# Causal attention and a mixture of experts on one core: attention in blocks of four heads and 512 queries, a select in place of the mask matmul, the residual added at the end, the first eight expert tiles loaded during attention

## The chip, the core and the metric

The kernel runs on one core of a Trainium2 chip. Its engines work side by side and meet through semaphores: PE (TensorE), DVE (VectorE), ACT (ScalarE), POOL (GpSimd) and SP, which issues DMAs. The metric is the device time of one execution in microseconds; several runs are taken and their median is compared. One more execution is taken with the hardware profiler, and all rows below are from it.

## The reference

x is 1024 tokens of 256 numbers, in float32. What is computed:

```python
xn = layernorm(x)
q, k = rope(xn @ wq.T), rope(xn @ wk.T); v = xn @ wv.T      # 16 heads of 16
scores = q @ k.T / sqrt(16), masked with -inf where key > query
attn_out = softmax(scores) @ v, heads joined, @ wo.T
s = softmax(xn @ gate_weight.T)                             # 64 experts
w, e = top_k(s, 8); w = w / sum(w)
moe = sum over the 8 experts: w * (silu(xn @ w_gate[e]) * (xn @ w_up[e])) @ w_down[e]   # inner size 96
out = x + attn_out + moe
```

## The kernel before

**Preparation.** The 1024 tokens are eight tiles (NT) of 128. They are normalised, transposed, and multiplied with the weights of q, k, v and the gate. q and k are rotated, transposed and split into a high and a low part, which SP stores to memory (`store_parts`, once for each half of the tokens) and loads again in another order (`stage`, five DMAs for a head group and half). The 16 heads are four groups (G) of four heads (HG). `qz` and `kz` hold a group's queries and keys with head size, parts and extra rows along the partitions; there are three pairs (SLOTS), so group 3 takes the pair of group 0. `set_ones` and `clear_max_rows` fill the extra rows, of which POOL zeroes the surroundings first (L608).

**Attention.** The maximum of each query's scores is needed before the exponential. It is found by a pass of its own: PE multiplies 128 queries with up to 512 keys (`max_scores`, L832, 192 matmuls), DVE takes the maxima (`use_max`: L1156 with the causal mask added, L1159 where no mask is needed). A transpose and two DVE operations give the negated maxima of one group and half (`use_neg`), and SP writes them as two rows of `qz` (`place_negmax`, L440), so that the score matmul subtracts them itself. The second pass goes by steps of one group and one tile of keys: PE computes keys times queries (`scores`, L851, up to 512 queries a matmul, 192 matmuls), adds a causal mask with a bf16 matmul at each diagonal (L854, 128 of them), ACT takes the exponential (L683) into `probs` (two buffers of four heads and 1024 queries), and PE multiplies with v (`pv`, L873) into two banks (L867 fills them with zeros first). After each group ACT copies the sums out (`att_out`, L691), PE transposes (L883), DVE divides by the row sums (L1180, L1181). Order: all eight key tiles of a group from the last to the first, the diagonal with the smallest width first. `attention_order` deals the maximum units out over the steps; before the first score step it makes all of group 0 and AHEAD = 48 units of work more. All A units (maxima, negations, posts, the routing table's spread, att and out) share three PSUM banks in turn and are used by DVE in the same order.

**Routing.** DVE finds the top 8 (L1061 to L1067), PE counts (`counts`, L810 and L813), DVE makes slot numbers and tile tables, POOL scatters the token rows to `slots` in 64 indirect DMAs (L616). The experts' rows are cut into tiles of 128, in this run 90.

**Transition and experts.** The first half of the output projection (128 of the 256 features) runs in the last group's steps, the second half after it (L939, L944, L1222), and with it x becomes the residual in `x_sb`, which SP stores to `y_acc[0]` (L504). POOL's first addition waits for that store. The tiles' rows lie in the place of `v_aug`, their weights in that of `probs`; the first eight tiles' rows and weights are loaded when those are free, by SP. A tile then goes: transpose (L955), copy on DVE (L1238), gate and up (L964), tanh on ACT (L723), products on DVE (L1242, L1246), down (L971), weighting on ACT (L729), and POOL adds the rows to one of four accumulators in memory by indirect DMA (L627). Each of four result buffers is used again when its addition has landed. At the end SP loads the four accumulators (L526, L530) and DVE sums them (L1270, L1274).

## Time and profile before

| | |
|---|---|
| median of 3 runs | 463.66 us (463.17 to 465.8) |
| profiled execution | 461.81 us |
| its span, first to last instruction | 459.7 us |
| PE busy | 364.3 us, 79% |
| DVE busy | 277.5 us, 60% |
| POOL busy | 238.7 us, 52% |
| ACT busy | 168.8 us, 37% |
| DMA | 92.96 MB, 202 GB/s in the mean |

Busy shares are means over three stages that look quite different; a slice of the page's second part is 11.5 us, a digit is a tenth of it. The digits of PEclk are the granted clock in tenths of 2.4 GHz. Durations of matmuls hold their way through the array, so neighbours overlap: what one costs is read from start to start.

### The profile page before, as it was taken

To read this page: it belongs to the slowest core of one execution; us is meant where nothing else is said; L and a number is where in the kernel's file an instruction comes from. 1 tells how busy PE (TensorE), PEld (TensorE's weight loads), DVE (VectorE), ACT (ScalarE), POOL (GpSimd) and SP (SyncE) were. 2 spreads that over 40 slices of the span, in tenths; PEclk is the share of its full clock that TensorE was granted. 3 is DMA by queue.
4 is the path that set the end of the run, shared out by engine and by line. 5 is a ranking of instruction groups with operands and counts; after the bars stand their busy time and mean duration, and the time that the engine had idled before them with its cause. 6 is when DMAs were issued, how large, how long until landed. Compare 5 with 4: busy or idle time off the path is not lost.

```text
span 459.7 us, 9456 instructions
## 1 busy us (share of the span) xinstructions
PE 364.3 (79%) x2230; PEld 248.4 (54%) x2234; DVE 277.5 (60%) x1083; ACT 168.8 (37%) x413; POOL 238.7 (52%) x194
## 2 busy tenths in 40 slices
PE   2695958599999999989997788887888888778600
PEld 1253625255545545544535777776776777677400
DVE  7783687968777987731404556665656656556506
ACT  1132200036545554666672333333333333333300
POOL 3769060007777777000000577868787877777720
PEclk9898875669999999999999989999999999999955
DMA  6038797373358333000047899999999999999997
GB/s 200 0 127 237 205 193 164 145 283 117 136 178 275 132 131 130 16 3 1 1 116 231 234 276 278 299 283 280 306 301 291 302 307 261 281 289 275 292 256 257
DMA packets 72512, 92.96 MB, mean 202 GB/s; under 512 B 8648, under 2 KB 62504, under 8 KB 72488
## 3 DMA queue, kind: packets, MB, share of 16 engines
q1 hardware_dynamic: 46312, 61.59, 43.1%
q0 software_dynamic: 16032, 22.29, 23.2%
q10 hardware_dynamic: 10144, 8.79, 5.9%
q8 instruction: 11, 0.18, 0.2%
q14 instruction: 13, 0.11, 0.1%
HBM read 58.92 MB, written 33.46 MB: 201 GB/s over the span
## 4 chain that ended last, share of the span: by engine, by line
PE 34%; DMA 25%; DVE 16%; issue 12%; POOL 8%; ACT 3%; DVEq 1%; POOLq 1%; SPq 1%; ACTq 0%
DMA y_acc<-att_raw,dst 19%; PE ps L851 9%; PE ps L832 8%; PE ps L873 7%; POOL y_acc L627 7%; DVE ps L1156 3%; DVE mx_low L1159 3%; DMA probs<-y_acc 2%; PE ps L854 2%; PE ps L776 2%; ACT att_raw L729 1%; ACT probs L683 1%; DMA qk_parts<-probs 1%; DMA kz<-ones 1%; DMA y_acc<-x_sb 1%
## 5 line engine op out<-in xcount | busy, mean ns | idle before, releaser
L627 POOL DMA_INDIRECT y_acc<-att_raw,dst x90 | 139.8, 1553 | 117.6 <-ACT att_raw L729 86.9
L683 ACT ACTIVATE probs<-ps 128x128 f32<-128x128 f32 (+3 forms) x192 | 84.1, 491 | 93.0 <-PE ps L854 91.3
L964 PE MATMUL ps<-att,probs 128*96 128x128 f32 x720 | 95.1, 275 | 4.5 <-issue 2.6
L964 PEld LDWEIGHTS ps<-att,probs 128*96 128x96 f32 x720 | 88.5, 165 | 14.8 <-issue 7.4
L616 POOL DMA_INDIRECT slots<-rows,slot_i x64 | 61.7, 964 | 56.5 <-DVE rows L1094 37.3
L832 PE MATMUL ps<-kz,qz 128*128 128x512 f32 (+3 forms) x192 | 71.2, 441 | 18.9 <-DVE mx_low L1159 10.2
L971 PE MATMUL ps<-probs,hidden_sb 96*128 96x256 f32 x180 | 59.5, 412 | 29.2 <-DVE hidden_sb L1246 25.6
L729 ACT ACTIVATE att_raw<-ps,w_slot 128x256 f32<-128x256 f32 x90 | 42.6, 473 | 83.0 <-DVE dst L1232 52.7
L851 PE MATMUL ps<-qz,kz 128*128 128x128 f32 (+3 forms) x192 | 70.0, 420 | 1.0 <-ACT probs L683 0.6
L1156 DVE CUSTOM_DVE_ANT_0 ps<-ps,mask_qk 128x512 f32<-128x512 f32 (+3 forms) x128 | 61.0, 504 | 10.5 <-PE ps L832 10.2
L832 PEld LDWEIGHTS ps<-kz,qz 128*128 128x128 f32 x192 | 39.2, 213 | 42.1 <-DVE mx_low L1159 21.1
L1230 DVE SCALAR_TENSOR_TENSOR w_junk<-v_aug,tile_exp 128x8 f32<-128x8 f32 x90 | 20.4, 227 | 63.3 <-DMA y_acc<-att_raw,dst 62.6
L1159 DVE TENSOR_REDUCE mx_low<-ps 128x1 f32<-128x512 f32 x64 | 44.1, 689 | 21.1 <-PE ps L832 20.2
L851 PEld LDWEIGHTS ps<-qz,kz 128*128 128x128 f32 x192 | 37.3, 198 | 31.7 <-ACT probs L683 19.6
L971 PEld LDWEIGHTS ps<-probs,hidden_sb 96*128 96x128 f32 x180 | 27.2, 191 | 40.3 <-DVE hidden_sb L1246 36.1
L1238 DVE COPY att<-ps 128x256 f32<-128x256 f32 x92 | 38.9, 424 | 11.3 <-PE ps L955 5.8
L873 PE MATMUL ps<-probs,v_aug 128*32 128x512 f32 (+3 forms) x384 | 40.9, 501 | 0.2 <-ACT probs L683 0.2
L723 ACT ACTIVATE att<-ps 96x128 f32<-96x128 f32 x90 | 24.5, 273 | 41.3 <-PE ps L964 37.4
L955 PE MATMUL ps<-ident,v_aug 128*128 128x128 f32 x184 | 35.2, 274 | 0.0
L854 PE MATMUL ps<-mask_kq,ident_b 128*128 128x128 bf16 x128 | 30.0, 236 | 0.0
L1246 DVE TENSOR_TENSOR hidden_sb<-att,ps 96x128 f32<-96x128 f32 x90 | 25.4, 283 | 4.0
L1242 DVE SCALAR_TENSOR_TENSOR att<-att,ps 96x128 f32<-96x128 f32 x90 | 24.6, 273 | 0.0
(142 smaller groups left out, 314.7 us busy)
## 6 DMA issues: line engine op xcount, KB each, us to landing
probs<-w_gu SPq DMA_DIRECT2D x96, 192.0 KB, 5.3
v_aug<-slots SPq DMA_DIRECT2D x96, 160.0 KB
probs<-w_down ACTq DMA_DIRECT2D x88, 96.0 KB
y_acc<-zero SPq DMA_DIRECT2D x12, 384.0 KB, 4.2
qk_parts<-probs SPq DMA_DIRECT2D x4, 1024.0 KB, 6.2
qz<-qk_parts SPq DMA_DIRECT2D x16, 256.0 KB, 6.9
probs<-y_acc SPq DMA_DIRECT2D x3, 1024.0 KB, 8.7
kz<-qk_parts SPq DMA_DIRECT2D x8, 256.0 KB, 5.5
```

The costliest lines, as they stand in the source:

```text
L616: pool.indirect_dma_start(slots[:, :], bass.IndirectOffsetOnAxis(ap=slot_i[:, t, k:k + 1], axis=0), rows[:, t, :], None).then_inc(s_scat, 16)
L627: pool.indirect_dma_start(y_acc[u][:, :], bass.IndirectOffsetOnAxis(ap=dst[u][:, 0:1], axis=0), y_sb[u], None, compute_op=ALU.add).then_in ...
L683: act.activation(probs[:, step % 2, j, lo:hi], ps[:, B_BANKS[n % len(B_BANKS)], lo % HALF:(hi - 1) % HALF + 1], ACT.Exp, scale=DK ** -0.5) ...
L729: act.activation(y_sb[u], ps[:, 4 + b, 0:D], ACT.Copy, scale=w_slot[u][:, 0:1]).then_inc(s_y, 1)
L832: pe.matmul(bank[:, 0:width], head_rows(qz, g, j, i, P), kz[g % SLOTS][0:P, lo // HALF, j, 0:width], start=True, stop=True).then_inc(s_ap, 1)
L851: last = pe.matmul(bank[:, a:b], head_rows(kz, g, j, kt, P), qz[g % SLOTS][0:P, lo // HALF, j, a:b], start=True, stop=True, skip_group_che ...
L854: last = pe.matmul(bank[:, a:a + P], ident_b[:, :], mask_kq[:, :], start=False, stop=True, skip_group_check=True)
L873: last = pe.matmul(ps[VW * j:VW * (j + 1), PV_BANK + lo // HALF, lo % HALF:(hi - 1) % HALF + 1], v_aug[:, kt, g * HG + j, :], probs[:, ste ...
L964: last = pe.matmul(ps[0:I, 2 + b, w * P:(w + 1) * P], wgu[u][:, (2 * c + w) * I:(2 * c + w + 1) * I], xgT[b][:, c * P:(c + 1) * P], start= ...
L971: pe.matmul(ps[:, 4 + b, 0:D], hh[b], wdn[u], start=True, stop=True).then_inc(s_dn, 1)
L1156: dve.tensor_tensor_reduce(bank, bank, mask_qk[:, HALF - width:HALF], 1.0, TAKEN, ALU.add, ALU.max, mx[:, g % 2, i // CT, j, i % CT:i % CT ...
L1159: dve.reduce_max(mx_low[:, g % 2, j, i % CT:i % CT + 1], bank, AX.X).then_inc(s_ad, 1)
```

## The change

- Attention goes by eight blocks of one group and one half of the queries (512), in the order BLOCKS: (0,0), (1,0), (2,0), (0,1), (1,1), (2,1), (3,0), (3,1). A block of half 0 has four key tiles, one of half 1 eight, from the first to the last; 48 steps as before, with the same matmuls for scores and maxima. The sums of a block use one of two banks, alternately, and start with `start=True`, without zeroing.
- The mask matmuls are gone. After the exponentials of a diagonal step POOL sets the future keys to zero in `probs` (`cut_future`), ahead of the scatters in its queue. `pv` of a step comes two steps later (LAG) and waits for the cut. `probs` has four slots of 512 queries.
- The maxima are made 24 units ahead of the scores, growing to 40 units. Projections of v for tiles 2 to 7 come before the first maximum. Top-8 work, counts, ranks and tables are dealt over steps 1 to 22, the scatters over the steps from 12 on.
- The output projection is done with both halves of the features, four tiles in steps 43 to 45, four after the last block. The result is added to `x_sb`, which is no longer stored; DVE adds it to the first accumulator at the end.
- Expert rows and weights get a place of their own, over `qz1` and `kz1`, and the first eight tiles are loaded once block (1,1) is done and all scatters have landed.

```diff
-AHEAD = HG * 12
-FIRST_STEPS = 6
+BLOCKS = ((0, 0), (1, 0), (2, 0), (0, 1), (1, 1), (2, 1), (3, 0), (3, 1))
+AHEAD = 24
 NEG_LAG = 2
+LAG = 2
+P_SLOTS = 4
+CHOOSE_STEP, RANK_STEP, WEIGHT_STEP = 1, 9, 12
+TILE_STEPS = (14, 16, 18, 20, 22)
+OUT_STEP = 43
...
+    for m, (g, c) in enumerate(BLOCKS):
+        units = [("max", g, i, j, u) for i in range(c * CT, (c + 1) * CT) for j in range(HG)
+                 for u in range(len(a_units(i)))]
+        lag = 0 if m == 1 else NEG_LAG
+        if m:
+            units.insert(lag, ("neg",) + BLOCKS[m - 1])
+        stream += units
+    stream.append(("neg",) + BLOCKS[-1])
...
+    for s in range(len(B_STEPS) + LAG):
+        extra = others(s)
+        if s < len(B_STEPS):
             for j in range(HG):
+                n = s * HG + j
+                ahead(AHEAD + n + min(max(n - 32, 0) // 1, 16))
+                order.append(("b", s, j))
+                if j == 1 and s >= LAG:
+                    order.append(("pv", s - LAG))
+                if j % 2 == 1 or s == len(B_STEPS) - 1:
+                    order += extra[:1]
+                    extra = extra[1:]
+            order += extra
+        else:
+            order.append(("pv", s - LAG))
...
@@ SP
             set_ones(0)
+            stage(1, 0)
+            set_ones(1)
             store_parts(1)
             sp.wait_ge(s_parts[1], 32)
             stage(0, 1)
-            stage(1, 1)
-            stage(1, 0)
-            set_ones(1)
             place_negmax(0, 0)
             sp.wait_ge(s_vlog, NT)
             sp.wait_ge(s_rot, NT)
             set_ones(2)
+            stage(2, 0)
+            place_negmax(1, 0)
+            stage(1, 1)
             stage(2, 1)
-            stage(2, 0)
+            place_negmax(2, 0)
+            zero_scratch()
             place_negmax(0, 1)
-            zero_scratch()
...
+            place_negmax(1, 1)
+            sp.wait_ge(s_bp, HG * (last_step(BLOCKS.index((0, 1))) + 1))
+            clear_max_rows(0)
+            stage(3, 0)
+            stage(3, 1)
+            place_negmax(2, 1)
+            place_negmax(3, 0)
+            place_negmax(3, 1)
...
+            sp.wait_ge(s_bp, HG * (last_step(BLOCKS.index((1, 1))) + 1))
             first_tiles = numbers(0)
-            sp.wait_ge(s_pv, (G - 1) * NT + done)
...
-            sp.wait_ge(s_res, NT // 2)
-            sp.dma_start(y_acc[0][0:N, :].rearrange("(t p) d -> p t d", p=P), x_sb[:, :, :]).then_inc(s_resd, 16)
...
@@ POOL
+            def cut_future(s):
+                first = queries(s)[0]
+                diagonal = probs[:, s % P_SLOTS, :, first:first + P]
+                pool.wait_ge(s_be, HG * (s + 1))
+                pool.affine_select(out=diagonal, in_=diagonal, compare_op=ALU.is_ge, fill=0.0, base=0,
+                                   pattern=[[0, HG], [1, P]], channel_multiplier=-1).then_inc(s_cut, 1)
+            pairs = [(t, k) for t in range(NT) for k in range(K)]
+            for s in range(len(B_STEPS)):
+                if on_diagonal(s):
+                    cut_future(s)
...
+                if s >= WEIGHT_STEP:
+                    count = 1 + s % 2 if on_diagonal(s) else 3
+                    for t, k in pairs[:count]:
+                        scatter(t, k)
+                    pairs = pairs[count:]
...
-            pool.wait_ge(s_resd, 16)
...
@@ PE
+            def pv(s):
+                g, c, kt = B_STEPS[s]
+                m = BLOCKS.index((g, c))
+                lo, hi = queries(s)
+                pe.wait_ge(s_be, HG * (s + 1))
+                if on_diagonal(s):
+                    pe.wait_ge(s_cut, cuts_until(s))
+                if kt == 0 and m >= 2:
+                    pe.wait_ge(s_acc, m - 1)
...
-                    if lo == kt * P:
-                        last = pe.matmul(bank[:, a:a + P], ident_b[:, :], mask_kq[:, :], start=False, stop=True,
-                                         skip_group_check=True)
...
@@ DVE
             dve.wait_ge(s_yl[0], 16)
+            link(dve.tensor_tensor(sum_buf(0)[:, :, :], sum_buf(0)[:, :, :], x_sb[:, :, :], ALU.add))
```

## Rows read from the trace of the kernel before

**Rows 1.** The page's second part: granted clock of TensorE in 40 slices.
```profile
PEclk9898875669999999999999989999999999999955
```

**Rows 2.** First score matmul (line L851), then line L832's matmuls up to 96 us.
```profile
L851 PEld LDWEIGHTS ps<-qz,kz x192: 185/190/354, 95.7 to 239.1; 128*128 128x128 f32 x192
...
40.00:96.00 56.00, 29.96 (x62) 15.23 (x62) 0.68 0.76 203
```

**Rows 3.** Attention: length, busy of PE, PEld, DVE, ACT, POOL, clock, DMA.
```profile
93.00:243.00 150.00, 142.32 (x900) 76.05 (x904) 90.22 (x310) 87.38 (x197) 61.67 (x64) 0.97 0.34 116
```

**Rows 4.** POOL's additions: ns shortest/median/longest, first and last start.
```profile
L627 POOL DMA_INDIRECT y_acc<-att_raw,dst x90: 1550/1552/1592, 257.1 to 439.7; - x90
```

**Rows 5.** Timeline of the transition: start us, us, engine, line.
```profile
242.60 1.02 ACT L691 ACTIVATE att_raw<-ps 128x1024 f32<-128x1024 f32 x1 [2.04 <-PE ps L873]
...
251.43 1.08 PE L964 MATMUL ps<-att,probs 128*96 128x128 f32 x8 [0.72 <-DVE x_sb L1222]
...
254.49 0.47 ACT L729 ACTIVATE att_raw<-ps,w_slot 128x256 f32<-128x256 f32 x1 [0.58 <-PE ps L971]
...
257.12 1.59 POOL L627 DMA_INDIRECT y_acc<-att_raw,dst  x1 [73.21 <-ACT att_raw L729]
```

**Rows 6.** Timeline of the start; last two: DMA issues with us to landing.
```profile
40.90 1.10 SPq L413 DMA_DIRECT2D qk_parts<-probs  x2
42.65 3.51 POOL L608 MEMSET kz<- 64x4096 f32 x1 [0.15 <-POOL qz L608]
45.10 1.62 PE L832 MATMUL ps<-kz,qz 128*128 128x512 f32 x3 [4.85 <-DMA kz<-ones]
...
54.56 3.44 PE L776 MATMUL ps<-w_in_sb,xnT 128*128 128x320 f32 x12
...
qk_parts<-probs SPq DMA_DIRECT2D x4, 1024.0 KB, 6.2
...
qz<-neg_hi SPq DMA_DIRECT2D x1, 8.0 KB, 4.9
```

**Rows 7.** DVE's masked maxima: two in the timeline, then all of the line.
```profile
46.63 0.73 DVE L1156 CUSTOM_DVE_ANT_0 ps<-ps,mask_qk 128x512 f32<-128x512 f32 x1
...
47.28 0.73 DVE L1156 CUSTOM_DVE_ANT_0 ps<-ps,mask_qk 128x512 f32<-128x512 f32 x1
...
L1156 DVE CUSTOM_DVE_ANT_0 ps<-ps,mask_qk x128: 288/508/733, 46.0 to 199.0; 128x512 f32<-128x512 f32 x32, 128x384 f32<-128x384 f32 x32, 128x256 f32<-128x256 f32 x32, 128x128 f32<-128x128 f32 x32
```

**Rows 8.** PE in the timeline of attention; last: a product with V, from the chain.
```profile
150.07 0.23 PE L854 MATMUL ps<-mask_kq,ident_b 128*128 128x128 bf16 x1
150.11 0.48 PE L851 MATMUL ps<-qz,kz 128*128 128x512 f32 x1
150.43 0.40 PE L832 MATMUL ps<-kz,qz 128*128 128x512 f32 x1
150.67 0.27 PE L841 MATMUL ps<-ident,mx 128*16 128x128 f32 x1
...
188.73 0.99 PE ps L873 x8
```

**Rows 9.** A group of DVE's top-8 work, 60 to 93 us.
```profile
L1065 DVE FIND_INDEX8 top_i<-top_v,logits 128x8 uint32<-128x64 f32 x8 | 1.7, 218 | 0.0
```

**Rows 10.** Ten microseconds around the first score, columns as in rows 3.
```profile
90.00:100.00 10.00, 9.78 (x33) 5.58 (x33) 7.06 (x20) 2.02 (x7) 0.00 (x0) 0.50 1.02 395
```

**Rows 11.** POOL: the scatters, then the forms nearest to the cut.
```profile
L616 POOL DMA_INDIRECT slots<-rows,slot_i x64: 956/960/1212, 103.0 to 182.9; - x64
...
L583 POOL TENSOR_SCALAR_AFFINE_SELECT mask_qk<-mask_qk 128x512 bf16<-128x512 bf16 x1 | 0.6, 612 | 0.2 <-POOL mask_qk L581 0.2
...
L597 POOL TENSOR_TENSOR qk_rot<-rope_c,rope_s 128x512 f32<-128x512 f32 x8 | 10.4, 1302 | 5.7 <-DVE rope_s L1031 5.6 <-POOL qz L559 0.2
```

**Rows 12.** Timeline of the final sums on DVE.
```profile
448.74 2.29 DVE L1270 TENSOR_TENSOR probs<-probs 128x2048 f32<-128x2048 f32 x1 [11.39 <-DMA probs<-y_acc]
451.75 2.29 DVE L1270 TENSOR_TENSOR probs<-probs 128x2048 f32<-128x2048 f32 x1 [0.71 <-DMA probs<-y_acc]
```

473 lines of the change are left out of this document (203 added, 270 removed).

## The prediction

> **What bounds the kernel now.** I read the page's slices first, for the stages, and then a view of its own for each stage. The reader is to see three stages in them. Up to 95.7 us nothing is near its limit for long: TensorE's granted clock falls to 0.5 again and again [rows 1], and the first score matmul (L851) starts only at 95.7 us, because 62 of the 192 row-maximum matmuls (L832) are made before it [rows 2]. From there to the last product with V at 242.5 us TensorE is busy nearly throughout (142.32 us of the 150 from 93 us on) [rows 3]; DVE, ACT and POOL are not. From 257.1 us POOL adds one expert result after the other: 90 additions, the last issued at 439.7 us, one each 2.05 us, where the issue itself takes POOL 1.55 us, and most of the rest is the time until an earlier addition has landed and frees its buffer [rows 4]. Between the two, from 242.6 to 257.1 us, lies a transition [rows 5]. So the change can save in three places: before 95.7 us, in TensorE's work up to 242.5 us, and in the transition.
>
> **The start.** The first maximum waits for the constant rows, which land at 45.1 us [rows 6]; nothing before that moves. Now the six projections of V that were mixed in come first; three took 3.44 us [rows 6], so six take some 7 us from 40 us on; they are done at about 46.5 us and cost about 1 us beside that wait. Then 16 maxima: DVE takes 0.65 us from start to start for 512 columns (46.63 to 47.28), where the form runs 0.73 us, and its shortest, of 128 columns, 0.29 us [rows 7]; over the four widths I take 0.45 us, together 7 us, to 54 us. Transpose and negation add 1 us. The placement (two small DMAs) then has to pass SP's queue. There one more stage of group 1 and its ones now stand ahead of the second store. The ones wait for POOL's memset of kz1, which ends at 46.2 us [rows 6], so the store's two DMAs leave from 46.9 instead of 40.9 us. Their issue takes 1.1 us and they land 6.2 us later, at 54.2 us. Then five stage DMAs are issued in 2.7 us, and the placement, issued by 57.8 us, lands 4 to 5 us later behind that stage (4.9 us now [rows 6]). First scores: 62 us (58 to 66), 34 us earlier than now. Later placements stand behind stages too, and (0,1) behind the 13 zeroing DMAs (some 0.5 to 1 us of issue each); I find each of them issued in time, except that block 3's negation comes only three score units ahead of its use, against a round trip of some 5 us.
>
> **TensorE's work from the first score.** Before: 242.5 - 95.7 = 146.8 us. Edits:
> - 24 maxima are made ahead instead of 62, so 38 more lie in this stretch. One of 512 columns takes 0.24 us from start to start (150.43 to 150.67) beside a score matmul of 0.32 us [rows 8]; half of them are narrower or follow an idle moment. I take 0.27 us: +10.3 us (bounds 0.2 and 0.32: 7.6 to 12.2).
> - The 44 count matmuls of 64 columns come into the stretch, narrower than a mask matmul of 0.04 us (next point): +1 us.
> - 128 mask matmuls (L854) go. Their busy 0.23 us is mostly pipeline: the next matmul starts 0.04 us after one [rows 8]. -5 us (bounds -3 and -13, at 0.1 us each with their weights).
> - The zeroing matmuls (L867) and the wait ahead of them go: four times about 0.8 us, -3 us.
> - Projections, the posts and the first half of the output projection are as many as before.
> Sum 150.1 us. Of the old stretch 5 us ran at clock 0.5, which gives back 2.5 us: 147.6 us at full clock.
>
> **What is lost again.** First the clock: TensorE will have waited from 54 to 62 us, and in this kernel it was still at 0.50 through 90 to 100 us though it was busy for 9.78 us of the 10 [rows 10]. I take 12 us of half clock, +6 us. (The Trainium skill, "TensorE: Matmul & The Clock Gate", Part 1, says that the throttled state is the default and activity releases it; by that rule alone the half speed would end soon after the scores begin and the sum would be some 4 us lower. The row of 90 to 100 us speaks for the longer time, and I go by it.) Second DVE: in the first twelve steps TensorE's order asks for 64 maxima (24 of short blocks at 0.45 us, 20 reductions of 512 columns at 0.60, 20 others at about 0.4: 31 us), and for the top-8 work, the counts and ranks, now spread over these steps (eight times L1061, L1064 and L1065, of which L1065 alone is 1.7 us [rows 9], some 6 us in all; two passes over 128 x 512 and eight more maxima, 3 us; copies, scan and negations, 4.5 us), and two posts: 46 us. TensorE has 42 us there and 48 with the slow clock. Two engines that near each other don't overlap fully: +5 us. Third, waits for placements and for the chosen experts: +3 us. Together 147.6 + 14 = 161.6 us, so the last product ends at 62 + 161.6 = 223.6 us: 18.9 us earlier.
>
> **POOL in attention.** It gets 32 cuts (select on 128 x 512 f32), each ahead of queued scatters; a product waits for its cut two steps later, and behind it everything on TensorE. No row shows this form. Select on 128 x 512 bf16 took 0.61 us, and an addition of two 128 x 512 f32 tiles 1.30 us [rows 11]. I take 0.65 us, by the select rows, with 0.6 and 1.3 us as bounds. A long block holds 4 cuts and 18 scatters at 1.25 us (79.9 us for 64 [rows 11]): 22.5 + 2.6 = 25.1 us, 27.7 us at the upper bound. TensorE needs for such a block 32 scores (8.9 us), 8 products with V (6.7 us, 0.99 us for a full one [rows 8]), 32 maxima (8.9 us) and a post, some 26 us. So the cut costs nothing as long as POOL keeps up, and this cover is thin. The Trainium skill, "SBUF — State Buffer", section "SBUF: two separate sides", speaks against the cut: POOL and DVE take turns at a port pair for a whole instruction when DVE has two inputs in SBUF. DVE's maxima have one in PSUM, so the rule would stretch only a few cuts; no run here shows it yet. SP's first expert loads wait for all 64 scatters, and so does DVE's first att copy at step 43, with the output units behind it. The scatters end near step 41, some 14 us before the end. 24 loads at 0.55 us of issue (1.10 us for two [rows 6]) fill 13 us: the eight tiles are there in time.
>
> **Transition.** Before: 242.5 us to the first addition at 257.12 us, 14.6 us, of which the last 2.2 us wait for the residual's store (the result was ready at 254.96). After: att_out 0.6, post and normalise 1.5, then four transposes and four projections paced by DVE (8 x 0.42 us and their latencies, about 5 us), row transposes and copy 1.1, and gate_up to the first result 3.6 us as now (251.40 to 254.96) [rows 5]: 12.2 us. Gain 2.4 us. Loads ahead gain nothing more, since no gate_up waited for a weight.
>
> **Expert stage and tail.** The same 90 tiles, the same chain of additions: 0, bounds -5 and +3 us from how loads and additions meet. At the end x is added on DVE, 2.29 us like its neighbours. The sums start at 448.74 us, with the second buffer, and wait again for the third until 451.75 us, 3 us apart [rows 12]; so the first buffer is there near 445.7 us, and the extra addition fits ahead of 448.74 us. Cost 0; 2.3 us were that cover gone.
>
> **Sum.** 18.9 + 2.4 = 21.3 us. The profiled execution took 461.81 us with a span of 459.7 us; its time would become 440.5 us. It lies 1.85 us below the median of the runs shown, 463.66 us, so on that scale the forecast is 442.4 us.
>
> **Rivals.**
> 1. The first twelve steps are a chain of round trips: each block's negation, DMA and DVE's routing work follow one another, and half clock goes on. If each of the five early block borders costs 3 us more than I allow and the clock stays low for another 10 us (+5), 20 us are lost and 462 us come out; with two thirds of it 455 us, which I take as the rival's time. For it: the clock's digits in that stretch [rows 1], and DVE at 46 us of 48. Against: negations are made six units ahead. 18%.
> 2. It goes better: the clock rises soon and DVE and TensorE overlap as they do now, -6 to -10 us: 434 us. For it: TensorE held 95% from 93 to 243 us with DVE busy for 90.22 us of it [rows 3]. 20%.
> 3. Slower, by POOL. Its work from step 12 (about 114 us) to the last cut is 64 scatters (80 us) and 20 cuts. If a cut took x us with its waiting, the last one ends at 114 + 80 + 20x us. The kernel is slower from where attention ends after 247 us, at x = 2.6 us, twice the highest neighbour row; at 3.2 us it ends at 260 us: 478 us. For it: POOL is the slow engine elementwise and DVE shares its memory. Against: select at 512 columns is at 0.61 us, and each block leaves POOL idle time. 6%.
> 4. The loads in attention don't come early: scatters end late, DVE waits for them in front of the output units, and the transition grows to its old length or beyond by 5 us: 449 us. 8%.
> The forecast itself gets 48%.
>
> **How the numbers follow.** From 434 us less a few for the second rival to 455 us and a bit of the first: 430 to 457 us leaves out about 2 in 10. A measurement of this kernel can tell some 0.5% (2.3 us) from no change. Faster needs less than 461.3 us: forecast, second and fourth rival and nearly all of the first, 0.90. Within: 0.03, the tail of the first. Slower: the third and what the first leaves, 0.07.
>
> **What would show it.** First L851 near 62 us; TensorE busy over 90% from about 75 us on; no wait of L873 on POOL; cuts of 0.6 to 0.7 us; last product near 223 us; first addition 12 us after it; 182 us of additions; the x addition ending before the second load lands. Wrong it would be if the clock stays at 0.5 beyond 80 us, if products wait for cuts, or if additions take another time than 182 us.

## The result, and the profile after

The changed kernel takes 444.75 us in the median of four runs (441.88 to 446.57); the kernel before, beside it on the same chip, takes 464.73 us. The ratio is 0.956, with an interval of 0.948 to 0.964. Forecast were 442.4 us and 430 to 457.

The profiled execution took 446.54 us. The page of the changed kernel, its first two parts; slices are 11.1 us each:

```profile
span 444.8 us, 9127 instructions
...
PE 348.0 (78%) x2098; PEld 241.9 (54%) x2098; DVE 277.1 (62%) x1080; ACT 168.2 (38%) x415; POOL 259.3 (58%) x224
...
PE   2699839886998999889979888888888779788510
...
POOL 2759702110378787885204877777777667768720
PEclk9899758998699999999969999999999998989955
```

PE is busy 16.3 us less than before, POOL 20.6 us more (the 32 cuts). The attention stretch, where PE's digits are mostly 8 and 9, begins in the slice from 66.7 us instead of the one that holds 95.7 us.

The score matmuls and the additions of the changed kernel, from the views of their lines (first and last start after the durations in ns), which answer to [rows 2] and [rows 4]:

```profile
L886 PEld LDWEIGHTS ps<-qz,kz x192: 185/189/333, 65.7 to 221.1; 128*128 128x128 f32 x192
...
L661 POOL DMA_INDIRECT y_acc<-att_raw,dst x90: 1552/1554/1607, 239.0 to 426.1; - x90
```

| stage, profiled executions | before | after | difference |
|---|---|---|---|
| first score matmul | 95.7 | 65.7 | -30.0 |
| from it to the end of the last product with V | 146.8 | 157.3 | +10.5 |
| from there to the first addition | 14.6 | 16.0 | +1.4 |
| first to last addition | 182.6 | 187.1 | +4.5 |
| last addition to the end of the span | 20.0 | 18.7 | -1.3 |
| span | 459.7 | 444.8 | -14.9 |

So the gain is the earlier start of the scores, less what was moved out of that start into the stretch behind it. Everything after attention gave nothing in this execution. Most of its +4.5 us of additions is the execution's own: the same kernel, run once more, had 182.7 us there.

### The profile page after: what moved, and what is told of

It reads as the page before. It is cut to its first block, busy times and chain, and to the rows that moved or that the text cites. A ratio compares the mean times of both kernels' runs of the same rounds, so it can differ in the third digit from the quotient of the medians.

```text
span 444.8 us, 9127 instructions
## 1 busy us (share of the span) xinstructions
PE 348.0 (78%) x2098; PEld 241.9 (54%) x2098; DVE 277.1 (62%) x1080; ACT 168.2 (38%) x415; POOL 259.3 (58%) x224
## 4 chain that ended last, share of the span: by engine, by line
POOL 25%; DMA 22%; PE 18%; issue 17%; DVE 13%; ACT 2%; SPq 1%; DVEq 1%; POOLq 1%; ACTq 0%
DMA y_acc<-att_raw,dst 15%; POOL slots L627 10%; POOL y_acc L661 8%; PE ps L886 3%; PE ps L900 3%; DVE ps L1160 3%; DMA probs<-y_acc 2%; DMA qz<-neg_lo 2%; PE ps L849 2%; PE ps L964 2%; DMA qk_parts<-probs 2%; PE ps L929 2%; DVE mx_low L1163 2%; PE ps L957 2%; POOL qk_rot L612 2%
## 5 line engine op out<-in xcount | busy, mean ns | idle before, releaser
L717 ACT ACTIVATE probs<-ps 128x512 f32<-128x512 f32 (+3 forms) x192 | 85.1, 493 | 86.3 <-PE ps L886 85.0
L957 PE MATMUL ps<-att,tile_bufs 128*96 128x128 f32 x720 | 96.1, 277 | 3.6 <-issue 2.5
L957 PEld LDWEIGHTS ps<-att,tile_bufs 128*96 128x96 f32 x720 | 89.5, 166 | 14.0 <-issue 6.8
L964 PE MATMUL ps<-tile_bufs,hidden_sb 96*128 96x256 f32 x180 | 60.2, 417 | 31.7 <-DVE hidden_sb L1239 28.1
L1160 DVE CUSTOM_DVE_ANT_0 ps<-ps,mask_qk 128x128 f32<-128x128 f32 (+3 forms) x128 | 61.4, 505 | 24.7 <-PE ps L849 22.2
L886 PE MATMUL ps<-qz,kz 128*128 128x512 f32 (+3 forms) x192 | 68.0, 373 | 10.8 <-DMA qz<-neg_lo 9.8
L627 POOL DMA_INDIRECT slots<-rows,slot_i x64 | 62.1, 971 | 19.5 <-issue 17.0
L635 POOL TENSOR_SCALAR_AFFINE_SELECT probs<-probs 128x512 f32<-128x512 f32 x32 | 20.5, 640 | 65.8 <-ACT probs L717 65.6
L1223 DVE SCALAR_TENSOR_TENSOR w_junk<-tile_bufs,tile_exp 128x8 f32<-128x8 f32 x90 | 20.3, 226 | 61.4 <-DMA y_acc<-att_raw,dst 60.9
L964 PEld LDWEIGHTS ps<-tile_bufs,hidden_sb 96*128 96x128 f32 x180 | 27.8, 195 | 42.0 <-DVE hidden_sb L1239 37.8
L900 PE MATMUL ps<-probs,v_aug 128*32 128x512 f32 (+3 forms) x384 | 42.2, 512 | 1.8 <-POOL probs L635 1.8
L948 PE MATMUL ps<-ident,tile_bufs 128*128 128x128 f32 x184 | 35.6, 276 | 0.5 <-DVE x_sb L1205 0.5
```

The costliest lines, as they stand in the source:

```text
L627: pool.indirect_dma_start(slots[:, :], bass.IndirectOffsetOnAxis(ap=slot_i[:, t, k:k + 1], axis=0), rows[:, t, :], None).then_inc(s_scat, 16)
L717: act.activation(probs[:, s % P_SLOTS, j, lo:hi], ps[:, B_BANKS[n % len(B_BANKS)], lo:hi], ACT.Exp, scale=DK ** -0.5).then_inc(s_be, 1)
L886: pe.matmul(ps[:, B_BANKS[n % len(B_BANKS)], lo:hi], head_rows(kz, g, j, kt, P), qz[g % SLOTS][0:P, c, j, lo:hi], start=True, stop=True).t ...
L900: last = pe.matmul(ps[VW * j:VW * (j + 1), PV_BANKS[m % 2], lo:hi], v_aug[:, kt, g * HG + j, :], probs[:, s % P_SLOTS, j, lo:hi], start=(k ...
L957: last = pe.matmul(ps[0:I, 2 + b, w * P:(w + 1) * P], wgu[u][:, (2 * c + w) * I:(2 * c + w + 1) * I], xgT[b][:, c * P:(c + 1) * P], start= ...
L964: pe.matmul(ps[:, 4 + b, 0:D], hh[b], wdn[u], start=True, stop=True).then_inc(s_dn, 1)
```

## The experiments

Three chips did the twelve runs. Each group below ran on one of them, beside the kernel before, and chips differ: the kernel before took 462.1 us on the first, 537.9 on the second and 540.6 on the third. Times are compared within a group only. Between the groups the text compares differences, and says so. Where this section gives the length of a transition, it counts from the start of the last product with V (16.2 us in the first profile of the changed kernel); the table above counts from its end, 0.2 to 0.3 us later.

### First group: where the time of the attention stretch goes

Kernel before: 462.13 us (seven runs). The changed kernel once more:

> The changed kernel once more, as the neighbour of the other three, since its own profiled execution took 446.54 us and its other executions 441.88 to 446.57 us. Both theories expect the same of it: 443 to 446 us, first score matmul near 66 us, last product with V near 223 us. If the time from the first to the last addition is again near 187 us (before: 182.5 us), the longer expert stage belongs to the change; if it lies at 182 to 184 us, it was that execution's own.

Measured: 441.51 us (439.89 to 445.09), ratio 0.963 (0.953 to 0.973). In its trace the scores start at 63.9 us, the last product with V at 221.2, and the additions run from 237.4 to 420.1 us: 182.7 us, where [rows 4] gave 182.6 and the first execution 187.1. So the first execution's 4.5 us are not a fixed cost of the change. But the thirteen traces of the changed kernel and its variants lie from 182.2 to 188.7 us, 185.3 in the mean, and the kernel before has one trace; whether the change costs the stage a little in the mean isn't shown. The transition is 16.2 us again.

**Is the granted clock what costs?** Sixteen idle matmuls ahead of the wait for the first placement, whose bank is written afresh later:

```diff
+                if n == 0:
+                    for _ in range(16):
+                        pe.matmul(ps[:, PV_BANKS[0], :], zero_b[:, :], mask_qk[:, :], start=True, stop=True)
                 if j == 0 and kt == 0:
                     pe.wait_ge(s_negd[g % SLOTS][c], 32 * (g // SLOTS + 1))
```

> TensorE makes 16 idle matmuls of 512 columns into an unused bank while it waits for the first placement (58 to 66 us, clock 0.5). Theory (the slow clock at the first scores costs 4 to 6 us, as the prediction's sum has it): the clock is at 1.0 when the scores begin, the first twelve steps shorten and the time falls by 3 us or more. Rival (DVE paces those steps, so the clock matters little there): within 1.5 us of the changed kernel.

Measured: 440.78 us (437.52 to 444.13), ratio 0.962 (0.953 to 0.970). Windows of the repeated kernel and then of this one (busy time of PE, PEld, DVE, ACT, POOL, granted clock, DMA):

```profile
60.00:70.00 10.00, 6.03 (x17) 5.08 (x17) 4.43 (x19) 4.21 (x8) 0.64 (x1) 0.54 0.64 131
70.00:110.00 40.00, 31.84 (x212) 17.81 (x212) 35.64 (x148) 16.07 (x41) 6.36 (x10) 0.96 0.58 177
...
225.00:230.00 5.00, 4.89 (x14) 3.94 (x15) 1.91 (x5) 0.00 (x0) 0.00 (x0) 0.54 0.24 81
```

```profile
60.00:70.00 10.00, 6.44 (x27) 3.74 (x29) 6.21 (x29) 4.37 (x10) 1.27 (x2) 0.92 0.58 122
70.00:110.00 40.00, 31.73 (x210) 17.61 (x202) 33.72 (x135) 15.15 (x38) 5.71 (x9) 0.93 0.58 177
...
225.00:230.00 5.00, 4.48 (x24) 3.35 (x22) 2.36 (x6) 0.00 (x0) 0.00 (x0) 1.00 0.10 35
```

The clock from 60 to 70 us rose from 0.54 to 0.92, TensorE did ten more matmuls there, four of them idle ones, and the last product with V starts at 221.1 us against 221.2: nothing came of it. Where the lead went can be seen. The first score was at 62.6 us, 1.3 us earlier, and then TensorE met a wait that the repeated kernel does not have:

```profile
68.50 0.47 PE L849 MATMUL ps<-kz,qz 128*128 128x128 f32 x1 [1.65 <-DMA qz<-qk_parts]
...
74.94 0.51 PE L889 MATMUL ps<-qz,kz 128*128 128x512 f32 x1 [0.43 <-DMA qz<-neg_lo]
```

The stage of block (2,0) lands at 68.5 us. The order has two maxima of that block ahead of the negation of block (1,0), so the placement of (1,0) and the first score of the second block hang on this stage too. That score starts at 74.94 us here and at 75.33 us in the repeated kernel. From 76 to 100 us, at clock 1.00, DVE is busy for 21.8 of 24 us in the repeated kernel and TensorE for 19.5, so there DVE is the nearer bound. And the slow clock was not all gone: from the first score on TensorE was at half clock for 6.8 us (68.4 to 71.9, behind the wait for the stage, and 102.6 to 106.0), against 12.1 us in the repeated kernel. What the rest costs was not tried.

The last rows of the windows tell another thing. In this execution the transition too ran at clock 1.00, and took 13.8 instead of 16.2 us. Its projections, first in the repeated kernel, then here:

```profile
225.11 2.04 PE L929 MATMUL ps<-w_out_sb,rows 128*128 128x256 f32 x4 [0.18 <-DVE rows L1199]
...
227.37 1.91 PE L929 MATMUL ps<-w_out_sb,rows 128*128 128x256 f32 x4
```

```profile
224.73 1.10 PE L932 MATMUL ps<-w_out_sb,rows 128*128 128x256 f32 x4 [0.39 <-DVE rows L1202]
...
225.88 1.03 PE L932 MATMUL ps<-w_out_sb,rows 128*128 128x256 f32 x4
```

2.0 against 1.1 us for the same four matmuls, the two levels of the clock. There the clock is on the path. Why sixteen matmuls at 60 us kept it up at 225 us these rows don't say. It differs between executions whose transition is the same: 16.2 us at a mean clock of 0.79 (four traces, three of them of the changed kernel itself), 15.0 to 15.4 us at 0.89 (four variants), 13.8 us here at 1.00. A later run puts idle matmuls into the transition itself.

**What do the cuts cost?** The cuts and the waits for them are left out, so future keys of the diagonal tiles count in the sums of this kernel. (POOL then waits for the routing table itself, before it reads its count of tiles.)

```diff
-                if on_diagonal(s):
-                    cut_future(s)
...
-                if on_diagonal(s):
-                    pe.wait_ge(s_cut, cuts_until(s))
```

> The 32 cuts on POOL and the waits for them are left out, so that keys after the query in the diagonal tiles count too; everything else is as in the changed kernel. POOL loses 20 cuts of 0.64 us and their gaps from the stretch of the scatters, 16 us in all. Theory (POOL's cover is thin but holds, TensorE is the bound): 1 to 4 us less. Rival (POOL is the bound of attention from 118 to 208 us, as the chain of the changed kernel shows it at 34.5% of 110 to 245 us): last product 10 us or more earlier, and the time less by 8 us or more.

Measured: 437.84 us (435.94 to 439.64), ratio 0.951 (0.944 to 0.959): 3.7 us less than with them. The cover is thin, as the forecast said, and not whole. The cuts, and a product that waits for one, from the view of line L635 and the timeline of the first profile of the changed kernel:

```profile
L635 POOL TENSOR_SCALAR_AFFINE_SELECT probs<-probs x32: 629/636/662, 69.4 to 221.8; 128x512 f32<-128x512 f32 x32
...
184.54 1.06 PE L900 MATMUL ps<-probs,v_aug 128*32 128x512 f32 x8 [1.12 <-POOL probs L635]
```

The repeated kernel waits 1.7 us in two places of L900 for cuts up to 225 us, and 3.0 us in one place (DVE's copy for the output units, L1199) for scatters. The last scatter is issued at 206.0 us there and at 195.5 without cuts. That makes 4.7 us of waits, and the medians are 3.7 us apart; the four times of one kernel do not overlap those of the other, the intervals of the ratios do a little. The traces give less: from the first score to the end of the last product 155.6 us without cuts against 157.6, and the first score, ahead of any cut, came 1.1 us earlier by chance. So the cuts cost some 2 to 4 us.

**Can the first placement leave earlier?** It stands behind SP's wait for the second store. It is put ahead of that wait:

```diff
             store_parts(1)
+            place_negmax(0, 0)
             sp.wait_ge(s_parts[1], 32)
             stage(0, 1)
-            place_negmax(0, 0)
```

> SP places the negated maxima of block (0,0) before it waits for the second store, not behind that wait and a stage. In the changed kernel they were ready at about 55.3 us, issued at 59.47 and 60.09 us and landed at 65.6 us. Theory (the start is bound by what stands ahead of the placement in SP's queue): the first score moves from 65.7 to about 58 us and everything up to the expert stage with it, 5 to 8 us less in all. Rival (DVE's work in the first twelve steps is the bound, it was busy 9.3 us of 10 from 70 us on): the first score moves, but the first twelve steps get longer by as much, and the time falls by under 2 us.

Measured: 447.16 us (442.13 to 449.27), ratio 0.969 (0.959 to 0.980). The first score comes 7.5 us earlier, at 56.4 us, and the last product 3.0 us later, at 224.2. Neither side had reckoned with what TensorE then met, a wait for the third block's queries. From its timeline, first TensorE's row and then SP's queue:

```profile
68.70 0.47 PE L849 MATMUL ps<-kz,qz 128*128 128x128 f32 x1 [7.33 <-DMA qz<-qk_parts]
```

```profile
54.55 0.60 SPq L468 DMA_DIRECT2D qz<-neg_lo  x1
...
57.11 1.06 SPq L456 DMA_DIRECT2D qz<-qk_parts  x2
...
59.00 1.69 SPq L449 DMA_DIRECT2D kz<-qk_parts  x3
60.73 1.07 SPq L456 DMA_DIRECT2D qz<-qk_parts  x2
```

Block (2,0) is staged last, issued by 61.8 us, and its maxima, 24 units ahead of the scores, ask for it at 61.4 us. An earlier first score moves the whole stream of maxima forward, and into a transfer that nobody had waited for. It cost 7.3 us, nearly all that had been won: the second block's first score starts at 75.16 us, against 75.33 in the repeated kernel. Why the rest came 3 us later still is not settled. Two things are seen in the trace: the third block's first score waits 2.25 us for its placement instead of 1.31, and from the first score on TensorE is at half clock for 22.6 us instead of 12.1. This was also the slowest of the kernel's four executions, 449.27 us.

### Second group: the queue, the lead, the loads, the residual

Kernel before: 537.87 us (seven runs). This group has no run of the unaltered changed kernel; the runs are read against each other, above all against the late loads and the store, which alter nothing before the last product.

**Both transfers early**, the cure for the last run: the placement and the stage of (2,0) ahead of the wait.

```diff
             store_parts(1)
-            sp.wait_ge(s_parts[1], 32)
-            stage(0, 1)
             place_negmax(0, 0)
             sp.wait_ge(s_vlog, NT)
...
             set_ones(2)
             stage(2, 0)
+            sp.wait_ge(s_parts[1], 32)
+            stage(0, 1)
```

> As the kernel that placed block (0,0)'s maxima first, and now SP also issues the ones and the stage of group 2, half 0, before it waits for the second store, since that stage reads only the first store. In the kernel before this one TensorE stood still for 7.3 us until 68.7 us for exactly that stage, and the first score at 56.4 us gained nothing. Theory (the start is a chain of SP's queue and the DMAs in it, whichever comes last): the wait goes, first score near 57 us, 3 to 6 us less than the changed kernel (441.5 us in the last comparison). Rival (DVE is the bound of steps 0 to 11, busy 9.3 us of 10 from 90 us on): what is gained by 75 us is lost by 118 us, within 2 us of the changed kernel.

Measured: 475.23 us (473.27 to 479.18), ratio 0.883 (0.879 to 0.886). The first score comes at 59.3 us, where the late loads and the store have it at 65.3 and 63.9, and the last product starts at 257.9 us against 256.1 and 255.0. The wait of 7.3 us is halved, not gone:

```profile
68.22 0.33 PE L849 MATMUL ps<-kz,qz 128*128 128x128 f32 x1 [3.60 <-DMA qz<-qk_parts]
```

Of the lead 1.1 to 2.6 us are left at 120 us (by the same exponential in the three traces), and the rest is lost behind that, where the stalls begin that the third group tells of. This trace is of the slowest of its four executions. The median is 2.1 us under that of the late loads, and the intervals overlap; so the order may be worth some 2 us, which isn't shown.

**The lead of the maxima.** 64 units ahead at all times instead of 24 growing to 40:

```diff
-                ahead(AHEAD + n + min(max(n - 32, 0) // 1, 16))
+                ahead(max(64, AHEAD + n + min(max(n - 32, 0) // 1, 16)))
```

> 64 row maxima are made ahead of the first score, as the kernel before made 62, until the changed kernel's own order has caught up at unit 36; nothing else differs. Theory (the gain of the change is the early first score, with maxima on DVE beside scores on TensorE): first score near 85 us, some 8 to 14 us slower than the changed kernel. Rival (the gain comes from the blocks, the missing mask matmuls and the short transition, and the order of maxima only moves the same work about): within 3 us.

Measured: 491.37 us (486.25 to 494.69), ratio 0.911 (0.904 to 0.917), some 12 to 16 us over the others of this group. The first score is at 85.9 us, some 21 us later, and the last product starts at 269.8 us, 14 later. Two windows of it, up to the first score and after:

```profile
50.00:86.00 36.00, 26.25 (x57) 14.90 (x58) 27.49 (x108) 0.00 (x0) 4.45 (x2) 0.51 0.74 186
86.00:110.00 24.00, 22.32 (x163) 11.70 (x163) 12.46 (x64) 17.03 (x44) 6.37 (x10) 0.95 0.46 181
```

Ahead of the scores ACT has nothing to do and TensorE runs at 0.51; after them TensorE is at 22.3 of 24 us. So the short lead is worth some 14 us. The 21 us by which the first score came later are not lost whole, since the maxima made ahead of it are missing behind it, as the sum of the forecast had it. This kernel is still 46.5 us faster than the kernel before on this chip, so here the lead is only a part of the gain; on the first chip, where the whole gain is 20.6 us, the lead was not varied.

**The loads in attention.** SP waits for the last product with V before it issues the first eight tiles:

```diff
+            sp.wait_ge(s_pv, len(B_STEPS))
             first_tiles = numbers(0)
```

> SP issues the first eight expert tiles only after the last product with V (223 us) instead of from 212 us on. In the changed kernel the first gate and up matmul starts at 234.6 us and a load lands 4.4 us after its issue, three issues a tile at 0.52 us each. Theory (the loads in attention buy nothing, the output projection covers them): within 1.5 us of the changed kernel. Rival (the loads ahead are what shortens the transition): the first addition 5 us or more later, and the time with it.

Measured: 477.32 us (475.92 to 478.6), ratio 0.888 (0.884 to 0.891). From the start of the last product to the first addition 16.6 us pass, against 16.2 with the loads inside attention wherever the clock was as low (0.79). The first two runs of this group have 15.0 and 15.2 us, but at 0.89. The first load leaves at 257.74 us, and no gate and up matmul waits for one. At the same clock the early loads are worth 0.4 us, about the nothing that the forecast said.

**The residual.** It is stored to the first accumulator again, ahead of the first addition, and the last addition on DVE is left out:

```diff
+            sp.wait_ge(s_zeroed, 16 * (3 * NY + 1))
+            sp.wait_ge(s_ad, len(a_order))
+            sp.dma_start(y_acc[0][0:N, :].rearrange("(t p) d -> p t d", p=P), x_sb[:, :, :]).then_inc(s_resd, 16)
...
+            pool.wait_ge(s_resd, 16)
...
-            link(dve.tensor_tensor(sum_buf(0)[:, :, :], sum_buf(0)[:, :, :], x_sb[:, :, :], ALU.add))
```

> The residual is stored to the first accumulator again, POOL's first addition waits for that store, and DVE's addition of x at the end is left out: the way of the kernel before, in the changed kernel. The last x tile is ready at 233.5 us and the store took 4.4 us, so it lands at about 238.4 us, where the first addition started at 239.0 us. Theory: within 1 us, first addition at 239 to 240 us, and the first sum at the end may start as early as before. Rival (the missing store is worth the 2.2 us that the first addition waited before): 2 us or more slower.

Measured: 479.51 us (477.84 to 485.7), ratio 0.891 (0.887 to 0.895). The transition is 17.3 us, 1.1 more than the changed kernel's at nearly the same clock. From the first weighted result to the first addition 1.9 us pass, in all the runs without the store 0.8. So the store costs about 1 us; the forecast had put all of the old 2.2 us on it.

### Third group: the mask, and the parts together

Kernel before: 540.55 us (eleven runs). The changed kernel for the third time:

> The changed kernel again, as the neighbour of the other three. On one chip all executions of the kernel before took 537 us and four variants of the changed one 475 to 491 us, on the others 462 and 441 us; this says on which kind of chip the three variants were run. First score at 64 to 66 us, transition 16 us at half clock.

Measured: 482.85 us (480.07 to 484.06, six runs), ratio 0.892 (0.888 to 0.896). Here the change is worth 57.7 us, on the first chip 20.6 us.

**The mask matmuls instead of the cuts**, all else as changed:

```diff
+                if on_diagonal(s):
+                    last = pe.matmul(bank[:, lo:lo + P], ident_b[:, :], mask_kq[:, :], start=False, stop=True,
+                                     skip_group_check=True)
...
-                if on_diagonal(s):
-                    cut_future(s)
...
-                if on_diagonal(s):
-                    pe.wait_ge(s_cut, cuts_until(s))
```

> The select is undone alone: the 32 cuts on POOL and their waits are gone and the 128 bf16 mask matmuls stand behind the diagonal score matmuls again. With neither cut nor mask the last product came 3.0 us earlier than in the changed kernel (218.2 against 221.2 us). Theory (a mask matmul costs 0.04 us): +4 us on TensorE after -3 us on POOL, in all within 2 us of the changed kernel; the select in itself brings almost nothing. Rival (the select is what shortens TensorE's stretch, at 0.1 us a mask): 5 us or more slower.

Measured: 522.78 us (518.09 to 525.73, six runs), ratio 0.966 (0.960 to 0.972), 39.9 us slower than with the cuts. Neither side had such a number. The profile shows what it is. The stretch of the scatters, 118 to 200 us, in windows of the changed kernel and then of this one:

```profile
118.00:200.00 82.00, 63.11 (x313) 32.24 (x313) 48.61 (x163) 36.68 (x75) 44.87 (x49) 0.85 0.33 107
```

```profile
118.00:200.00 82.00, 25.61 (x102) 11.16 (x101) 14.26 (x44) 11.23 (x21) 61.44 (x64) 0.60 0.34 126
```

Without cuts in its queue POOL issues all 64 scatters back to back. In that time TensorE does 102 matmuls instead of 313, and DVE and ACT stand still with it. The timeline of this kernel in the middle of it:

```profile
158.83 0.33 PE L895 MATMUL ps<-mask_kq,ident_b 128*128 128x128 bf16 x1
158.85 0.96 POOL L633 DMA_INDIRECT slots<-rows,slot_i  x1 [0.30 <-issue]
...
181.60 0.96 POOL L633 DMA_INDIRECT slots<-rows,slot_i  x1 [0.30 <-issue]
182.31 0.70 DVE L1168 CUSTOM_DVE_ANT_0 ps<-ps,mask_qk 128x512 f32<-128x512 f32 x1 [28.68 <-remote]
...
183.12 0.80 PE L854 MATMUL ps<-kz,qz 128*128 128x512 f32 x1 [23.96 <-issue]
...
188.49 0.60 ACT L722 ACTIVATE probs<-ps 128x512 f32<-128x512 f32 x1 [30.20 <-remote]
```

```profile
169.12 0.96 POOL L627 DMA_INDIRECT slots<-rows,slot_i  x1 [0.30 <-issue]
172.73 1.08 ACT L717 ACTIVATE probs<-ps 128x512 f32<-128x512 f32 x2 [9.38 <-remote]
...
182.80 0.63 POOL L635 TENSOR_SCALAR_AFFINE_SELECT probs<-probs 128x512 f32<-128x512 f32 x1 [12.72 <-ACT probs L717]
...
207.63 0.96 POOL L627 DMA_INDIRECT slots<-rows,slot_i  x1 [0.30 <-issue]
209.87 0.80 PE L849 MATMUL ps<-kz,qz 128*128 128x512 f32 x1 [8.78 <-issue]
```

The gaps cut the 64 scatters into three long trains, of 12, 14 and 14 (119.2 to 134.3, 152.6 to 170.1 and 191.2 to 208.6 us), and short ones of at most six. All seven traces with cuts from the two slow chips are alike in this: every "remote" wait above 2 us in attention begins 4 to 14 us into one of the three long trains and ends at most 2.7 us after it, and the short trains behind them have none. So the stalls go with the length of the train. The stops also fall on the same place of each engine's program (one on ACT follows its 129th instruction in all seven traces, though it ends at 167.5 us in one and at 180.8 in another). Since the scatters hang on the cuts, train and place move together, and these runs don't tell the two apart.

From 100 to 250 us ACT has 67.3 us of "remote" waits with mask matmuls and 17.5 us with cuts. None of the four traces of the first chip has one in the attention stretch, though the kernel without cuts issued its scatters there back to back as well, with TensorE busy in the same 82 us for this much:

```profile
118.00:200.00 82.00, 76.79 (x460) 40.68 (x459) 64.17 (x210) 52.67 (x118) 59.55 (x63) 1.00 0.45 154
```

So on the third chip the cuts instead of the mask matmuls are worth 40 us, of which by the price below some 6 us are the mask matmuls (an estimate) and the rest goes with the gaps in the train of scatters; on the first chip the same cuts cost 2 to 4 us. A kernel with neither cuts nor masks was not run on a slow chip. The variant with mask matmuls and an unbroken train is 17.8 us faster than the kernel before here, close to the change's whole gain on the first chip (20.6); this fits a kernel before that suffers the same stalls in its unbroken train of 64 scatters [rows 11]. No trace of the kernel before on this chip was taken, so that last step is argued, not shown.

What the run was made for, the price of a mask matmul, can be read where the scatters are over and TensorE has no waits. In this kernel, and then in the changed one:

```profile
272.50 0.34 PE L892 MATMUL ps<-qz,kz 128*128 128x384 f32 x1
272.68 0.23 PE L895 MATMUL ps<-mask_kq,ident_b 128*128 128x128 bf16 x1
272.72 0.47 PE L854 MATMUL ps<-kz,qz 128*128 128x512 f32 x1
```

```profile
230.53 0.34 PE L886 MATMUL ps<-qz,kz 128*128 128x384 f32 x1
230.71 0.40 PE L849 MATMUL ps<-kz,qz 128*128 128x512 f32 x1
```

From the score to the next maximum 0.22 us pass with the mask and 0.18 without: 0.04 us a mask matmul. All eight such places of this kernel have 0.21 to 0.22 us, all five of the other 0.17 to 0.18. With a product with V behind it (one diagonal score in four) a mask costs 0.07 us (0.34 against 0.27 us, three places each), and one place, at 293.9 us, has 0.15. An estimate from these for all 128: some 6 us.

**Idle matmuls in the transition, scatters from step 10.** With the sixteen of the second run, 3, 4 and four times 1 of the same kind around the last post, and `WEIGHT_STEP` 10:

```diff
-CHOOSE_STEP, RANK_STEP, WEIGHT_STEP = 1, 9, 12
+CHOOSE_STEP, RANK_STEP, WEIGHT_STEP = 1, 9, 10
...
+    order.append(("warm", 3))
     order.append(("post", m))
+    order.append(("warm", 4))
...
         order.append(("att", t))
+        order.append(("warm", 1))
```

> Meant to be better: 16 idle matmuls in the wait for the first placement, idle matmuls in the waits after the last product too (3, 4 and one behind each att transpose), and the scatters from step 10 instead of 12. In the run with only the first 16 the transition happened to run at clock 1.0 and took 13.8 us instead of 16.2. Theory: the clock holds through the transition (-2.5 us), scatters start and end some 6 us earlier, so DVE's 3.0 us wait for them at the first att copy and POOL's lateness go (-2 us): 3 to 6 us less than the changed kernel. Rival (the idle matmuls are in the way, and POOL's lateness was covered): within 1.5 us.

Measured: 482.2 us (480.66 to 488.4), ratio 0.891 (0.886 to 0.896): no gain. The transition did shrink, at clock 1.00, from 16.2 to 14.1 us, and the first addition came at 274.3 us instead of 277.3. The additions then took 187.7 us instead of 183.6. The first scatter came 11.5 us earlier (the long trains 1 to 6 us), and the last only 4.3 us earlier, at 241.0 us. ACT has 26.4 us of "remote" waits, where the changed kernel had 17.5.

**All together:** the queue's order of the second group's first run, and the edits of the last run with six idle matmuls at the start instead of sixteen.

```diff
-                    for _ in range(16):
+                    for _ in range(6):
```

> As the kernel before this one, and SP places the first maxima and loads group 2's stage before it waits for the second store, with 6 idle matmuls in the shorter wait. Theory (SP's queue binds the start, the 5 us that the first score gained on the slow chip carry through): 2 to 5 us less than the kernel before this one. Rival (DVE binds steps 0 to 11, and the gain is lost by 118 us): within 1.5 us of it.

Measured: 479.33 us (475.23 to 482.62), ratio 0.884 (0.880 to 0.889), 3.5 us under the changed kernel, with intervals that touch. Its profiled execution, the slowest of its six, had the last product at 263.5 us and 14.1 us of transition. It may be a little better; it isn't shown to be, and on the first chip it was not run.

## Why the prediction was right, and where its steps were off

**The start: right in kind, 3.7 us late.** The ones left at 46.35 us and the second store at 47.06, as worked out. The negated maxima were ready at 55.5 us, near the forecast's 55. What was mis-sized is the store: two issues took 2.1 us instead of 1.1, and it landed at 56.7, not 54.2 us. The stage went from there and the placement came behind it. SP's queue and the wait it ended, in the changed kernel:

```profile
56.68 1.58 SPq L449 DMA_DIRECT2D kz<-qk_parts  x3
58.30 1.06 SPq L456 DMA_DIRECT2D qz<-qk_parts  x2
59.47 0.58 SPq L468 DMA_DIRECT2D qz<-neg_hi  x1
60.09 0.59 SPq L468 DMA_DIRECT2D qz<-neg_lo  x1
...
65.66 0.79 PE L886 MATMUL ps<-qz,kz 128*128 128x512 f32 x1 [7.51 <-DMA qz<-neg_lo]
```

It looked like 7.5 us to be had. The run with the placement first shows that it isn't: 7.33 us of it come back as the next wait, for a stage that the negation of the second block hangs on.

**From the first score to the last product: 157.3 us, forecast 161.6.** The sum without losses was 147.6 us and the losses 14; measured are 9.7 over that sum, if the sum holds. Three of its terms can be judged.

The clock: TensorE was at 0.50 until 70.3 us and again from 104.5 to 107.9 and 111.3 to 118.1, 14.8 us where 12 were assumed. The 6 us for it are too much: the run with idle matmuls took 5.3 of 12.1 us of slow clock away, and moved the end by 0.1 us. (The Trainium skill, "TensorE: Matmul & The Clock Gate", Part 1, by which activity releases the clock, fits the first piece: the clock rose 4.6 us after the first score, not after the long time that [rows 10] had suggested. It does not tell the last one: from 112 to 118 us TensorE was busy for 6.00 of 6 us at 0.50.)

DVE: forecast was 46 us of work against 42 to 48; in the window from 70 to 110 us of the repeat it is at 35.6 of 40, above TensorE at 31.8. So the term was there, and the clock's lay in part beneath it, in part beneath the wait for the third block's stage.

The masks: 0.04 us each ahead of a maximum and 0.07 ahead of a product, so some 6 us where 5 stood. That term holds.

So the sum without losses stands at about 147 us, and it was the losses that were mis-sized: some 10 us instead of 14. The clock had too much, up to 6 us; the cuts, which stood at nothing, have 2 to 4 us; how the rest divides between DVE's pace, the later pieces of slow clock and the waits for placements (2.3 us in four places behind the first) the runs don't tell.

**The cuts.** Forecast were 0.65 us each; they took 0.636 (0.629 to 0.662), next to the bf16 select of [rows 11]. A rule of the Trainium skill ("SBUF — State Buffer", "SBUF: two separate sides") would have made some of them longer beside DVE. That was hardly tried: three of the 32 had a DVE instruction with two inputs in SBUF beside them, and took 0.642, 0.652 and 0.662 us; the others took up to 0.652. If there was an effect, it was at most 0.03 us. The nothing that they were to cost was 2 to 4 us on the first chip. The step that failed is the block's balance of 25.1 us on POOL against 26 on TensorE: it left out that a cut can't begin before its exponentials, which puts waits between the scatters (26.7 us in seven places of the repeat, from 100 to 225 us), and the copy behind the last scatter then waited 3.0 us.

**The transition: forecast 12.2 us, measured 16.0, 15.9 in the repeat.** Here the mechanism was missed. The eight projections were thought to be paced by DVE at 0.42 us each; in fact TensorE paced them: four matmuls of 256 columns for each tile, at half clock from 223.9 to 230.8 us. The clock fell there after two short gaps on TensorE, of 0.65 and 0.80 us. Timeline of the changed kernel, to be read against [rows 5]:

```profile
227.02 2.04 PE L929 MATMUL ps<-w_out_sb,rows 128*128 128x256 f32 x4 [0.18 <-DVE rows L1199]
...
229.10 0.42 DVE L1205 TENSOR_TENSOR x_sb<-ps,x_sb 128x256 f32<-128x256 f32 x1 [1.80 <-PE ps L929]
...
234.63 1.11 PE L957 MATMUL ps<-att,tile_bufs 128*96 128x128 f32 x8 [0.37 <-DVE att L1231]
```

2.4 us of the excess are the clock (from the start of the last product 16.2 against 13.8 at clock 1.00, and 14.1 twice on the third chip, with idle matmuls). By parts: from the last product to the first att transpose (225.75 us) 2.7 us where 2.1 were forecast, to the first gate_up 8.9 where 6.1 were, and to the first addition 4.4 where 3.6 were. The forecast's parts add up to 11.8, not 12.2. Its last part ended at the first result, and that took 3.6 us here too, until 238.19 us; the 0.8 us from the result to the addition had no term. In the kernel before they lay in the 2.2 us that were put down to the store. The gain of 2.4 us was a loss of 1.4.

**Expert stage and tail.** The stage was forecast at 182 us. It was 187.1 in the first execution, 182.7 in the repeat, and 182.2 to 188.7 over the others, so one execution can't show what the change does to it. The x addition was hidden, as worked out:

```profile
430.33 2.29 DVE L1261 TENSOR_TENSOR probs<-probs,x_sb 128x2048 f32<-128x2048 f32 x1 [7.79 <-DMA probs<-y_acc]
433.85 2.29 DVE L1264 TENSOR_TENSOR probs<-probs 128x2048 f32<-128x2048 f32 x1 [1.23 <-DMA probs<-y_acc]
```

The next sum still waits 1.23 us for its accumulator.

**The rivals.** The first, a chain of round trips, is not what came: there are few waits on placements, and the stretch ended earlier than forecast. The second, that it goes better, holds for the attention stretch alone, and there by 4.3 us where it named 6 to 10. The third needed cuts of 2.6 us. (Its own formula gives ends at 246 and 258 us, not 247 and 260; that changes nothing.) The fourth did not occur, as no load was waited for. The sum against the profiled execution, 440.5 us, is missed by 6.0: start +3.7, stretch -4.3, transition +3.8, additions +4.5, tail and what lies around the span -1.7. On the medians, 442.4 against 444.75, it is 2.4, since the profiled execution was slower than the median and the one before faster. The forecast was as near as that in part by luck: the stretch was overrated and the start, the transition and this execution's additions underrated, and the errors of the stretch and the start nearly cancel.

**What was to show it.** TensorE is busy for 133.1 of the 148 us from 75 us on, the 90% named. Wrong was that no product waits for a cut (1.8 us in two places), and the 12 us of transition.

## What to carry over

- Work moved from ahead of the first score to behind it fills the engines that stood idle ahead of it; but everything behind comes earlier too, and meets the next transfer sooner. In one run the first score came 7.5 us sooner and the wait for the next stage took it back.
- A short stage after a wait may run at half clock; its matmuls are to be priced at both levels. And a matmul's price is read over many places with it and without it: the mask cost 0.04 us in most, 0.07 ahead of a product, and 0.15 in one, so a single pair of rows can mislead.
- An operation that moves to another engine also changes the rhythm of that engine's queue. Here the cuts cost 2 to 4 us on one chip; on another the kernel with them was 40 us faster than the one with mask matmuls, of which the masks explain some 6.

## What the runs showed of the hardware

Chips of the same kind differ by far more than the change: the kernel before took 462.1 us on one and 537.9 and 540.6 us on two others, the changed kernel 441.5 and 482.9. On the two slow ones TensorE, DVE and ACT stop together while POOL issues indirect DMAs at 1.26 us intervals, and not on the first, with the same instructions at the same intervals. In one train of 64 the stops last up to 24 to 30 us; they begin 12 us after the first scatter and end 10 us after the last is issued. With trains of 12 to 14 they last up to 11 us and end at most 2.7 us after the train, and trains of six or fewer have none above 2 us. What the three engines wait for no row names, and it was not tried apart from the scatters: a run with the scatters spread evenly, or issued without work beside them, would be the next one. Until that is known, a gain measured for this kernel on one chip is not a gain on the next: the ratio of the same two programs was 0.963 on one and 0.892 on the other.
